# Two attention phases and two FFN phases in one kernel: another order of the attention heads' tasks, and other counts of PSUM banks in the second attention phase

## What is computed

```python
x = x + attn_a(layernorm(x))   # 32 heads of 16, 8 key/value heads, rotary, causal
x = x + ffn(layernorm(x))      # 4-bit codes with scales plus a low-rank part, SiLU gate
x = x + attn_b(layernorm(x))   # 32 heads of 16, 32 key/value heads, with biases, causal
x = x + ffn(layernorm(x))
```

## Time and profile before

| | us |
|---|---|
| median of 3 runs (lowest, highest) | 2064.7 (2063.78, 2068.85) |
| the profiled execution, its own time | 2070.07 |
| its span | 2068.0 |
| head of aa, until its first scores | 0 to 59.3 |
| head of ab, until its first scores | 946 to 1006.5 |
| four batches of ab's pairs | to 1695 |
| PE busy | 1787.6, 86% of the span |
| DVE, ACT, POOL busy | 58%, 45%, 36% |
| granted PE clock, mean | 0.939 |

### The profile page before, as it was taken

How to read it: one execution, slowest core, us unless ns; L and a number is a source line. 1 busy time by engine, 2 the same in 40 slices (tenths; PEclk the granted TensorE clock), 3 DMA queues, 4 the chain that set the end, 5 groups by cost and what they waited for, 6 DMA issues and landing times. The chain is left out here.

```text
span 2068.0 us, 35964 instructions
## 1 busy us (share of the span) xinstructions
PE 1787.6 (86%) x12624; PEld 1293.8 (63%) x12624; DVE 1200.0 (58%) x2474; ACT 935.2 (45%) x1740; POOL 745.5 (36%) x2278
## 2 busy tenths in 40 slices
PE   5889989899859999994788898888889875999997
PEld 4556666556436777773566666666666644777775
DVE  5787787777637555433656545655654544754543
ACT  3555455455525454331544434544443533544542
POOL 3545454454402122122444534544543420311311
PEclk8999999999979999996898998999999987999999
DMA  2000100100044201103001000100001006311010
GB/s 103 1 2 2 62 1 22 42 1 27 17 139 142 82 6 56 41 5 135 1 1 32 1 32 1 32 7 27 22 1 42 1 1 186 115 61 42 20 41 21
DMA packets 47033, 81.27 MB, mean 39 GB/s; under 512 B 6666, under 2 KB 18570, under 8 KB 46868
## 3 DMA queue, kind: packets, MB, share of 16 engines
q1 hardware_dynamic: 46868, 79.13, 12.0%
HBM read 62.34 MB, written 16.78 MB: 38 GB/s over the span
## 5 line engine op out<-in xcount | busy, mean ns | idle before, releaser
L247 PE MATMUL f_ring<-f_xt,f_codes 128*128 128x512 f32 (+1 forms) x1408 | 361.3, 399 | 6.6 <-DVEq L1399 5.5
L247 PEld LDWEIGHTS f_ring<-f_xt,f_codes 128*128 128x128 f32 (+1 forms) x1408 | 264.4, 188 | 76.3 <-DVEq L1399 6.2
L1257 POOL TENSOR_TENSOR f_ht<-f_work,f_ht 128x512 fp32r<-128x512 f32 (+1 forms) x88 | 114.7, 1307 | 473.6 <-ACT f_ht L1317 473.6
L852 DVE TENSOR_REDUCE ab_nmax<-ab_maxima 128x1 f32<-128x384 f32 (+1 forms) x256 | 152.5, 621 | 137.7 <-PE ab_maxima L964 134.6
L748 ACT ACTIVATE aa_region<-aa_scores 128x512 f32<-128x512 f32 x320 | 184.9, 599 | 104.5 <-PE aa_scores L1001 102.8
L748 ACT ACTIVATE ab_region<-ab_scores 128x512 f32<-128x512 f32 x320 | 183.2, 604 | 80.3 <-PE ab_scores L1001 78.1
L626 POOL TENSOR_SCALAR_AFFINE_SELECT ab_region<-ab_region 128x128 f32<-128x128 f32 x512 | 140.7, 299 | 180.9 <-ACT ab_region L748 180.1
L1410 DVE TENSOR_TENSOR f_work<-f_ring,f_work 128x512 f32<-128x512 f32 (+1 forms) x176 | 120.6, 690 | 146.4 <-ACT f_work L1306 117.9
L1306 ACT ACTIVATE f_work<-f_ring,f_scales 128x512 f32<-128x512 f32 (+1 forms) x176 | 120.8, 687 | 171.8 <-PE f_ring L247 171.3
L247 PE MATMUL f_ring<-f_dcodes,f_ht 128*128 128x512 f32 (+1 forms) x704 | 176.0, 405 | 10.3 <-DVE f_down_x L1380 9.3
L963 PE MATMUL ab_maxima<-ab_stacks 96*128 96x128 bf16 (+3 forms) x512 | 151.6, 325 | 37.8 <-DVE ab_nmax L852 33.7
(11 more groups left out here) (185 smaller groups left out, 3419.2 us busy)
## 6 DMA issues: line engine op xcount, KB each, us to landing
f_x<-mid SPq DMA_DIRECT2D x32, 256.0 KB, 4.1
f_raw<-mid SPq DMA_DIRECT2D x32, 256.0 KB, 4.4
f_raw<-in_gate_q SPq DMA_DIRECT2D x10, 512.0 KB, 6.2
f_raw<-in_up_q SPq DMA_DIRECT2D x10, 512.0 KB, 4.4
f_raw<-in_down_q SPq DMA_DIRECT2D x10, 512.0 KB, 3.7
aa_x<-in_x SPq DMA_DIRECT2D x16, 256.0 KB, 3.6
aa_res<-in_x SPq DMA_DIRECT2D x16, 256.0 KB, 3.0
mid<-aa_res SPq DMA_DIRECT2D x16, 256.0 KB, 2.0
```

The lines of the kernel that those rows point to most:

```text
L247: mm = pe.matmul(out, w, x, start=start and i == 0, stop=stop and i == len(pairs) - 1)
L852: last = dve.tensor_reduce(nm[:, qt, h:h + 1], src[:, 0:(qt + 1) * P], AX_X, ALU.max, negate=True)
L1257: pool.tensor_tensor(ht[0:r, LO, n, :], hid[0:r, n % 2, :], ht[0:r, HI, n, :].bitcast(F32), ALU.subtract).then_inc(hid_lo.sem, 1)
```

## The change

It changes the order of the two heads, the place of the other weights and of POOL's ones, ab's bank counts to 3 and 2, the order of DVE's work within a position of ab, and ab's table. Line numbers of the changed kernel are higher by 4 on PE and POOL and by 2 to 6 on DVE and ACT (L1092 becomes L1096, L837 becomes L843).

```diff
--- before.py
+++ after.py
@@ -381,7 +381,7 @@
     VHEADS = 4
     GROUPS = KU // VHEADS
     VSLOTS = 2 if rope else 5
-    MAXIMA, TASKS = (3, 2) if rope else (2, 3)
+    MAXIMA, TASKS = 3, 2
     table = Timetable(units, plan, head, TPARTS)
     HI, LO = 0, 1
 
@@ -502,7 +502,8 @@
         else:
             MAXIMA_AT = ((2, (0,)), (2, (1,)), (2, (2,)), (2, (3,)), (2, (4, 5)))
         FIRST_W = min(head_at("P"))
-        OTHER_W = [max(head_at("P")) + 2 + 2 * f for f in range(KD)]
+        OTHER_HI = (8, 10, 12, 13) if rope else (11, 12, 15, 16)
+        OTHER_LO = (15, 17, 19) if rope else (14, 15, 17)
         FIRST = sum(len(ks) for ahead, ks in MAXIMA_AT if ahead == 2)
         TRANSPOSE_AT, ROWS_AT, VALUES_AT = 2, 3, 4
 
@@ -594,10 +595,13 @@
 
         @block.gpsimd
         def _(pool):
-            pool.memset(stacks[MAXROW:ROWS, :, HU:NST, :], 1.0).then_inc(ones_set, 1)
-            pool.wait_ge(ones_set, 1)
-            pool.memset(v[:, :, :, :, HD:HD + 1], 1.0).then_inc(ones_set, 1)
-            pool.wait_ge(ones_set, 2)
+            def write_ones():
+                pool.wait_ge(rstd_made.sem, rstd_made.at(0, 2))
+                pool.sem_inc(waited, 1)
+                pool.memset(stacks[MAXROW:ROWS, :, HU:NST, :], 1.0).then_inc(ones_set, 1)
+                pool.wait_ge(ones_set, 1)
+                pool.memset(v[:, :, :, :, HD:HD + 1], 1.0).then_inc(ones_set, 1)
+                pool.wait_ge(ones_set, 2)
 
             def split_max(b, s):
 
@@ -645,6 +649,8 @@
                         pool.wait_ge(var_made.sem, var_made.at(b0 + bb, t + 1))
                         pool.tensor_tensor(rstd[:, t:t + 1], var[:, t:t + 1], power[:], ALU.pow)\
                             .then_inc(rstd_made.sem, 1)
+                    if region is table.head and pos == head_at("X")[1] - 1:
+                        write_ones()
                     for _, bb, u, t in table.started(region, pos, 3 if rope else 2, "P"):
                         k = u * NT + t
                         r = rest[:, k % 2, :]
@@ -704,9 +710,9 @@
                     if region is table.head:
                         if pos == FIRST_W:
                             first_weights()
-                        if pos in OTHER_W:
-                            other_weights(OTHER_W.index(pos))
-                        if pos == OTHER_W[-1] + 1:
+                        if pos in OTHER_HI:
+                            other_weights(OTHER_HI.index(pos))
+                        if step is not None and region[0][pos - 1] is None:
                             if biased:
                                 act.wait_ge(extra_made, 1)
                             act.wait_ge(w_lo_made, 1 + KD)
@@ -890,22 +896,18 @@
                     if region is table.head:
                         if pos == FIRST_W:
                             first_weights()
-                        if pos in OTHER_W:
-                            other_weights(OTHER_W.index(pos))
+                        if pos in OTHER_LO:
+                            other_weights(OTHER_LO.index(pos))
                     if step is not None:
                         bs, s, i = step
                         b = b0 + bs
                         if i == ROWS_AT and (after := following(region, b, s, 1)) is not None:
                             max_rows(*after)
-                        if not rope:
-                            maxima_of(region, b, s, i)
                     for _, bb, _, n in table.started(region, pos, 1, "F"):
                         finish(where, b0 + bb, n)
                     for _, u, t, p in table.turned(region, pos, 1):
                         if p == 0:
                             stack_out(dve.tensor_copy, dve, where, u, t, p)
-                    if not rope:
-                        tokens_of(region, pos, b0)
                     for kind, bb, _, t in table.started(region, pos, 1, "X", "C"):
                         src, tok = banks.read(dve, where, (kind, 0, t, 0)), slice(t * P, (t + 1) * P)
                         if kind == "X":
@@ -929,18 +931,21 @@
                             rotate(where, b0 + bb, u, t)
                         else:
                             remainder(where, b0 + bb, u, t)
+                    if step is not None:
+                        maxima_of(region, b, s, i)
+                    tokens_of(region, pos, b0)
                     if rope:
-                        if step is not None:
-                            maxima_of(region, b, s, i)
-                        tokens_of(region, pos, b0)
                         for _, bb, u, t in table.started(region, pos, 2, "P"):
                             remainder(where, b0 + bb, u, t)
                     if step is None:
                         if region is table.head and region[0][pos + 1] is not None:
                             for k in range(6):
                                 reduce_max(0, 0, k)
-                            max_rows(0, 0)
                             for k in range(FIRST):
+                                if k == 3:
+                                    other_weights(KD - 1)
+                                if k == 4:
+                                    max_rows(0, 0)
                                 reduce_max(0, 1, k)
 
             whole(dve, part)
@@ -948,7 +953,6 @@
         @block.tensor
         def _(pe):
             THREE = ((HI, HI), (LO, HI), (HI, LO))
-            pe.wait_ge(ones_set, 2)
             pe.wait_ge(av_cleared, 1)
 
             def project(out, src, t, c0, n, bias_row):
@@ -1095,10 +1099,12 @@
                         if region is table.head and region[0][pos + 1] is not None:
                             banks.all_emptied(pe, where, [("T", 0, t, p)
                                                           for t in range(NT) for p in range(TPARTS)])
+                            pe.wait_ge(ones_set, 2)
                             for k in range(6):
                                 max_scores(0, 0, k)
-                            max_transposes(0, 0)
                             for k in range(FIRST):
+                                if k == 4:
+                                    max_transposes(0, 0)
                                 max_scores(0, 1, k)
                         if region is table.tail and region[0][pos - 1] is not None:
                             values(b0, QUADS - 1, False)
@@ -1594,22 +1600,22 @@
 )
 PLAN_B = timed(
     *[(20 * (u - 1) + j, "P", 0, u, t) for u in range(1, 4) for t, j in enumerate((0, 2, 4, 6))],
-    *CONTEXT,
-    *[(20 * (u - 1) + j, "T", 0, u, t) for u in range(1, 4) for t, j in enumerate((4, 6, 8, 10))],
+    *late(17, 10, "F"), *late(33, 20, "C"),
+    *[(20 * (u - 1) + j, "T", 0, u, t) for u in range(1, 4) for t, j in enumerate((5, 7, 9, 11))],
     *[(j, "O", -1, 0, t) for t, j in enumerate((14, 15, 16, 17))],
     *[(j, "X", 1, 0, t) for t, j in enumerate((50, 53, 56, 59))],
     *[(60 + j, "P", 1, 0, t) for t, j in enumerate((0, 2, 4, 6))],
-    *[(60 + j, "T", 1, 0, t) for t, j in enumerate((4, 6, 8, 10))],
+    *[(60 + j, "T", 1, 0, t) for t, j in enumerate((5, 7, 9, 11))],
 )
 HEAD_A = timed(
-    *[(3 + t, "X", 0, 0, t) for t in range(NT)],
-    *[(7 + 2 * t, "P", 0, 0, t) for t in range(NT)],
-    *[(14 + 2 * t, "T", 0, 0, t) for t in range(NT)],
+    *[(j, "X", 0, 0, t) for t, j in enumerate((3, 4, 7, 9))],
+    *[(6 + 2 * t, "P", 0, 0, t) for t in range(NT)],
+    *[(13 + 2 * t, "T", 0, 0, t) for t in range(NT)],
 )
 HEAD_B = timed(
-    *[(j, "X", 0, 0, t) for t, j in enumerate((3, 4, 8, 9))],
-    *[(11 + 2 * t, "P", 0, 0, t) for t in range(NT)],
-    *[(18 + 2 * t, "T", 0, 0, t) for t in range(NT)],
+    *[(j, "X", 0, 0, t) for t, j in enumerate((3, 4, 9, 10))],
+    *[(j, "P", 0, 0, t) for t, j in enumerate((6, 7, 12, 13))],
+    *[(j, "T", 0, 0, t) for t, j in enumerate((11, 13, 16, 18))],
 )
 
 
```

## The result

| | before | changed |
|---|---|---|
| median of four runs each (lowest, highest) | 2066.8 us (2063.8, 2073.1) | 2007.3 us (2004.6, 2009.2) |
| ratio, 95% interval | | 0.9707 (0.968 to 0.9734) |
| profiled execution: own time, span | 2070.1, 2068.0 | 2007.9, 2005.9 |
| PE busy; clock, mean | 1787.6 us; 0.939 | 1763.9 us; 0.950 |

It is 2.9% faster, 59 us in the medians and 62.1 in the spans; 62 was forecast. To see where they went, both spans are cut at five instructions: the first and the last scores of each attention phase, and DVE's first instruction of ab. Each row is of one profile.

What follows compares the result with a forecast made beforehand. PE, busy 86% of the span, bounds the kernel through its waits and low clock. Idle 25, clock 24, ab's head 5 and aa's head 8 sum to 62 us: 2003 us against the 2064.7 median, range 1968 to 2036.

Steps and rivals of the forecast that it cites:

- forecast case: Whole kernel: less idle time and a better clock in ab's batches, shorter heads; 2003 us, chance 0.50.
- The idle time in ab's batches: Ab's four batches: 61 us of PE's waits go, 36 us of new ones come, net 25 us less idle.
- Waits that go: Ab's batches: DVE's order and the slots remove 37 us, a third maxima bank 24 of 33.7; together 61 us.
- Waits that come: Ab's batches: two task banks and earlier transposes add F and T 27, X place 6, POOL's split 3; 36 us.
- POOL's split: Ab's batches: PE reaches max_transposes sooner and waits there for POOL; 3 us taken, 60 in all if aa's 23.1 come whole.
- The clock in ab: Ab's batches: 36 us lost at half speed; the 2.20 us gaps go, a third of the loss stays; gain 24 us.
- The head of ab: Ab's start to first scores: earlier P, mostly given back, then 2.5 us at the maxima and 2.5 before scores; 5 us saved.
- The step that failed: Ab's head: with POOL's ones behind two roots, P starts near 959 instead of 970.15, 11 us sooner.
- my row: Ab's head, profile before: POOL's copy of 0.30 us ran 1.95 beside DVE's other weights; 2 us given back before the maxima.
- The head of aa: Aa's start to first scores: P at about 15.4, T rounds 2.3 us shorter three times, 1 us before scores; 8 us saved.
- aa's body: Aa between its heads and ends: instruction order kept, so no change; 0 us.

Runs made afterwards that it cites:

- the last run on T and F: Ab's third and fourth T one slot later (10 and 12 of 20), against the 1965.6 us kernel with F at 8 and 18: 2020.2 us.
- another order: The kernel before with DVE's new order and the new slots for F and T in ab, banks and heads as before: 2020.8 us (0.9754).

## Why the prediction was right, and where it was not

Against 2003 (1968 to 2036) stood 2007.3. The forecast case is the one that happened in ab's batches; the heads failed.

- **The idle time in ab's batches: -25 forecast, -31 measured.** Waits that go: T behind the remainder 28.6 to 1.1, F behind the stacks 4.9 to 0, maxima 33.7 to 6.4 (10 taken). Waits that come: F behind the remainder 14 times 1.06, where I had 16 times 1.3; T behind F's work 8.0 for 6.4 (0.4 in 16 units); T behind X 5.9 for 6; POOL's split 3 more for 3. Not in the sum: X behind its normalisation went from 4.0 to 9.0. The order on DVE, which now has the normalisation's work last in the slot, is not the reason: with the order alone this wait is 3.1, with the new slots 4.9, and only with the new banks 9.7. T behind F's work (3.8 before) goes the same way: 0, 0 and 7.9.
- **The clock in ab: -24 forecast, -30 measured, by a step that is half right.** The step was that gaps of 2.2 us and more drop it and that one of 1.3, below aa's longest of 1.6, does not. For F's new wait it holds: behind none of its 14 waits of 1.06 us does the clock fall. But in the kernel before shorter waits dropped it too. In ab's stretch it fell in or right behind all eleven waits of T of 2.2 to 3.4 us, and also right behind two of three waits for a maxima bank of 2.1 us and seven of ten of 1.49. One of these, and its window:

```profile
1264.56 0.61 PE L963 MATMUL ab_maxima<-ab_stacks 96*128 96x512 bf16 x1 [1.49 <-DVE ab_nmax L852]
```

```profile
1264.00:1268.00 4.00, 3.44 (x13) 2.84 (x14) 2.41 (x5) 0.60 (x1) 1.47 (x7) 0.57 0.00 0
```

  So part of the clock's gain came with the maxima waits, which the term did not count, and the six falls within the changed kernel's stretch stand behind waits of 1.4 to 2.2 us. Nor is aa at 1.00 throughout: the earlier trace rows shows one batch of four, the last one has 0.97, and the changed kernel's four have 0.95 to 0.99. The number of short waits does not decide: DVE's order alone has 65 waits for a maxima bank, none above 1.0 us, and a clock of 1.00. The Trainium skill's rule against the term (TensorE: Matmul & The Clock Gate, "A second HAM failure mode: psum-queue depth-cycling") is not borne out by that run. The length of the longest wait does not decide alone either, as the last run on T and F shows: 0.96, with six of 13 falls behind pairs of 0.76 and 0.88 us, while the order with the new slots had waits of 2.0 us and 0.99.
- **What carries it.** The working priced the parts separately and never summed them by part of the change. By its own terms DVE's order gives 28.6 and the clock, and the banks and slots come to 24 and 8.7 against 36 of new waits, about nothing. The runs say the same of the sum: order alone 620.8, all three 619.4. They do not of its parts: the order alone also takes out the 8.7 (F behind the stacks, T behind F's work), and it brings 7.0 more of T behind POOL's copies (3.1 to 10.1) and 4.8 more of maxima waits, which no term had.
- **The head of ab: -5 forecast, +1.6 measured.** The step that failed: "POOL's ones (6.92 us) hold the first reciprocal roots; they now run behind two of them", with P near 959. The ones were priced at the roots alone and at nothing beside DVE. They held DVE's second normalisation for 7.32 us, and with them moved it takes about 0.55. Without that the forecast stands: with the ones out of the way P starts 12.9 us after the phase's start, for the 13 that I took, and the head is 55.3, for 55 to 56. The stretch of POOL's work by DVE, 2 us by my row, was 3.7 (4.09 less 0.43), beside two DVE pieces that followed each other without a gap.
- **The head of aa: -8 forecast, -5.0 measured.** The same step: P at 18.41 and not 15.4, by ones of 3.51 us. With the ones first P is at 15.45 and the first scores at 51.4, for 51.
- **aa's body: 0 forecast, +4.8 measured**, of the clock and within what the same instructions show.

The heads missed by 10, aa by 5 and the end phases by 3 the other way; ab's batches gave 12 more. That these cancel is luck, and the reasons for the idle time in the batches are what was right, with half of the step on the clock.

The Trainium skill states what the failing step lacked, in SBUF — State Buffer, section "Who interferes with whom": a DVE `tensor_scalar` can enter a 2-port mode, when its operands meet the conditions, and then it takes the interface pair that it shares with GpSimd; whichever of the two issues first has the pair for its whole instruction, and the other is fully blocked. The same section has DVE instructions with two SBUF inputs contend with a GpSimd instruction that reads SBUF, and not with one that only writes. The traces agree that they hold each other: 7.32 us for DVE's normalisation beside a POOL memset, 4.09 us for POOL's subtraction of two SBUF tiles beside DVE's. The recorded starts do not show the order: DVE's normalisation starts at 952.26 and POOL's memset at 952.38, and it was DVE that was held. No run here shows which mode DVE was in.

## What to carry to other kernels

Before moving a long write of one engine, look at what every engine does in the stretch that it moves to, not only at who waits for its result; here a write of 7 us on 3 partitions held DVE, and writing two bf16 numbers as one float32 halved it. Sum a change by its parts as well as by its waits, and time each part alone: one reordering on DVE was the whole gain of three edits, and one block moved on ACT, which the change did not touch, gave another 20 us. Compare idle time and busy time separately: between single profiles of the same instructions idle time repeated within 3 us here, while busy time moved by up to 11 with the clock. Behind a reordering in an engine's slot, list who waits for what is now last, here PE for the reductions, 4.8 us more.

## What the runs showed of the hardware that I had not expected

- A normalisation of 128x512 (0.54 us) took 7.32 us beside a POOL memset of 6.92, and 3.91 beside one of 3.51, while the batch statistics (0.69) and DVE's own memsets (0.48) ran at their usual length beside that memset in the kernel before.
- A memset of 3x8192 bf16 takes 6.92 us on POOL and 6.88 on DVE; the same bytes as 3x4096 float32 take 3.51 on POOL.
- The same instructions of aa took 512.5 to 521.3 us between their first and last scores, with PE busy for 459.3 to 470.5 of them: 4 us of difference between two single profiles say nothing by themselves.
- In the kernel before the clock fell in or right behind all eleven waits of PE of 2.2 us or more in ab's stretch, and behind seven of ten of 1.49; in the changed kernel behind none of 14 of 1.06.
- Moving two T's by one slot raised PE's idle time in ab from 32.9 us to 68.8, in waits of which none is above 2.2 us, and its busy time with it, by the clock, from 558.1 to 583.9; another order with 64.2 us of such waits (631.10 - 566.86) kept its clock at 0.99.
